# A graph network's edge blocks: the masks-times-weights products move to GpSimd, and two PSUM evictions to VectorE

## What is computed

```
z = _ln(x, ln1_g, ln1_b)
q = (z @ Wq + bq).reshape(L, H, D)
k = (z @ Wk + bk).reshape(L, H, D)
v = (z @ Wv + bv).reshape(L, H, D)
scores = einsum('ehd,ehd->eh', q[row], k[col]) * scale + bias
p = exp(scores - m[row])
alpha = p / segment_sum(p, row)[row]
out = segment_sum(alpha[:, :, None] * v[col], row)
```

## Time and profile before

| | before |
|---|---|
| median of 3 runs (lowest, highest) | 395.43 us (393.89, 395.63) |
| profiled execution, first to last instruction | 394.1 us |
| PE busy | 374.8 us, 95% |
| DVE busy | 312.1 us, 79% |
| ACT busy | 171.6 us, 44% |
| POOL busy | 4.2 us, 1% |
| stretch 22.0 to 104.2 us (fixed groups) | PE 81.1 of 82.2 us busy, DVE 80.2 |

### The profile page before, as it was taken

How to read it: one execution, slowest core, us unless ns; L and a number is a source line. 1 busy time by engine, 2 the same in 40 slices (tenths; PEclk the granted TensorE clock), 3 DMA queues, 4 the chain that set the end, 5 groups by cost and what they waited for, 6 DMA issues and landing times.

```text
span 394.1 us, 5108 instructions
## 1 busy us (share of the span) xinstructions
PE 374.8 (95%) x1786; PEld 282.2 (72%) x1786; DVE 312.1 (79%) x660; ACT 171.6 (44%) x287; POOL 4.2 (1%) x19
## 2 busy tenths in 40 slices
PE   2989999999999999999999999999999999999994
PEld 1545566666657888887678788887588878787773
DVE  5889999999848789897868976698875788388236
ACT  5664666563044234244559533262363530145410
POOL 4000000000000000000000000000000000000000
PEclk9999999999999999999999999999999999999988
DMA  7602444343135000068200512200600050000002
GB/s 238 250 1 69 152 154 141 105 153 112 52 112 183 1 2 0 2 215 315 111 2 1 172 43 101 114 0 0 211 4 0 2 180 33 2 0 0 2 12 94
DMA packets 16360, 32.92 MB, mean 84 GB/s; under 512 B 1360, under 2 KB 1488, under 8 KB 16336
## 3 DMA queue, kind: packets, MB, share of 16 engines
q1 hardware_dynamic: 15744, 32.25, 23.9%
q10 hardware_dynamic: 592, 0.36, 0.3%
HBM read 21.07 MB, written 1.05 MB: 56 GB/s over the span
## 4 chain that ended last, share of the span: by engine, by line
PE 77%; DVE 14%; ACT 4%; issue 2%; DMA 1%; DVEq 0%; ACTq 0%
PE acc L1395 11%; PE bank L1377 10%; PE bank L1480 7%; PE bank L1270 6%; PE bank L1271 6%; PE bank L1251 4%; PE acc L1251 4%; PE acc L1271 4%; PE acc L1270 4%; PE bank L1465 3%; PE acc L1451 3%; DVE big_rounded L652 2%; PE acc L1228 2%; PE bank L1228 2%; PE acc L1545 2%
## 5 line engine op out<-in xcount | busy, mean ns | idle before, releaser
L1395 PE MATMUL acc<-wide_rounded,c_rounded 128*126 128x512 f32 x200 | 59.5, 439 | 0.7 <-ACT acc L464 0.7
L1395 PEld LDWEIGHTS acc<-wide_rounded,c_rounded 128*126 128x126 f32 x200 | 36.9, 186 | 19.8 <-issue 13.0
L792 DVE TENSOR_SCALAR wide_rounded<-iota_f,picked 128x512 fp32r<-128x512 f32 x100 | 42.2, 480 | 1.5 <-issue 1.1
L483 ACT COPY z_sb<-acc 126x512 f32<-126x512 f32 x37 | 21.6, 585 | 42.0 <-PE acc L1395 33.3
L507 ACT ACTIVATE wide<-wide,low_col 128x512 f32<-128x512 f32 x32 | 21.3, 715 | 32.9 <-DVE low_col L905 32.8
L1480 PEld LDWEIGHTS bank<-v_sb,big 128*128 128x128 f32 x256 | 29.7, 192 | 4.7 <-issue 4.0
L625 DVE TENSOR_TENSOR wslot_rounded<-wslot,wide_rounded 128x512 fp32r<-128x512 f32 x24 | 16.2, 687 | 21.2 <-ACT wslot L377 21.2
L1480 PE MATMUL bank<-v_sb,big 128*128 128x65 f32 x256 | 31.6, 277 | 0.0
L798 DVE TENSOR_TENSOR c_rounded<-row_bc,wslot_rounded 128x1008 fp32r<-128x1008 bf16 x25 | 30.0, 1201 | 0.0
L1377 PE MATMUL bank<-t_sb,wslot 128*128 128x512 f32 x64 | 29.5, 594 | 0.5 <-ACT t_sb L459 0.5
L652 DVE TENSOR_TENSOR big_rounded<-big,big_rounded 128x1024 fp32r<-128x1024 f32 x24 | 29.1, 1221 | 0.5
(11 more groups left out here) (312 smaller groups left out, 769.6 us busy)
## 6 DMA issues: line engine op xcount, KB each, us to landing
big<-z_sb SPq DMA_DIRECT2D x36, 252.0 KB
big<-in_w SPq DMA_DIRECT2D x4, 2048.0 KB, 7.8
x_sb<-in_x SPq DMA_DIRECT2D x8, 256.0 KB, 4.6
big<-in_w_3t SPq DMA_DIRECT2D x2, 1024.0 KB, 6.7
row_bc<-in_rows SPq DMA_DIRECT2D x7, 256.0 KB, 6.4
wslot<-in_wq SPq DMA_DIRECT2D x1, 1024.0 KB, 8.9
wslot<-in_wk SPq DMA_DIRECT2D x1, 1024.0 KB, 10.7
wslot<-in_wv SPq DMA_DIRECT2D x1, 1024.0 KB, 12.8
```

The costliest lines, as they stand in the source:

```text
L483: nc.scalar.copy(stage[0:BROWS, b % STAGES, :], a).then_inc(S["staged"], 1)
L792: nc.vector.tensor_scalar(hot_ring[:, u, k, :], iota_f[:, :], picked[:, 0, s0 + k:s0 + k + 1], None, ALU.is_equal)
L1395: last = nc.tensor.matmul(to, st_ring[:, u, 2 * k + a, :, :].rearrange("p w k -> p (w k)"), hot_ring[:, u, k, :], start=False, stop=False, ...
```

## The change

`left_sides` becomes a function of the engine. For the 24 fixed groups GpSimd calls it, one instruction per group, in a loop of its own at the end of its program; the last group's product in the loop stays on VectorE. PE waits for two counters in place of one (`hots` from VectorE, `lefts` from GpSimd). VectorE evicts tiles 2 and 3 of the turned input instead of ScalarE, so it does two `tensor_scalar` of 128x512 from PSUM.

```diff
+        MASK_STEPS = {0: 5, RING: 8, 6: 9}
+        def left_sides(engine, u, s0):
+            c = slice(s0, s0 + GROUP)
+            return engine.tensor_tensor(
+                st_ring[:, u, :, :, :],
...
@@ gpsimd
+            pool.wait_ge(S["tables"], 7 + NT)
+            for g in range(NG - 1):
+                if g in MASK_STEPS:
+                    pool.wait_ge(S["round_steps"], MASK_STEPS[g])
+                if g >= RING:
+                    pool.wait_ge(S["pair_mm"], (g - RING + 1) * GROUP + 1)
+                left_sides(nc.gpsimd, g % RING, g * GROUP).then_inc(S["lefts"], 1)
@@ scalar
             clear(Z_BANKS[0])
-            z_turned(2)
-            z_turned(3)
             clear(Z_BANKS[1])
@@ vector
+            def z_turned(t):
+                dve.wait_ge(S["turned"], t + 1)
+                nc.vector.tensor_scalar(t_sb[:, t, :], bank[Z_BANKS[t]][:, :], colp("ln1_g", t), colp("ln1_b", t),
+                                        ALU.mult, ALU.add).then_inc(S["t_vector"], 1)
...
-            one_hots(0, 0, (2, 3))
+            one_hots(0, 0, (2, 3)).then_inc(S["hots"], 1)
             ln_coefs(1)
             for t in (0, 1):
                 ln_plain(1, t, h_sb)
-            left_sides(0, 0)
             slot_weights(5, later)
             dve.sem_inc(S["weights_read"], 1)
-            build(1, 1, GROUP)
+            dve.wait_ge(S["cols_in"], 16)
+            for t in (2, 3):
+                z_turned(t)
+            one_hots(1, GROUP).then_inc(S["hots"], 1)
...
             for g in range(RING, NG - 1):
-                build(g, g % RING, g * GROUP, (g - RING) * GROUP)
+                one_hots(g % RING, g * GROUP, freed=(g - RING) * GROUP).then_inc(S["hots"], 1)
...
             with nc.vector.Fori(0, trips) as j:
-                build(NG - 1, 0, FIXED, j * GROUP + (FIXED - RING * GROUP))
+                one_hots(0, FIXED, freed=j * GROUP + (FIXED - RING * GROUP))
+                left_sides(nc.vector, 0, FIXED).then_inc(S["built"], 1)
@@ tensor
             for g in range(NG - 1):
-                pairs(g, g % RING, held[GROUP * (g % 2):GROUP * (g % 2 + 1)])
+                pe.wait_ge(S["hots"], g + 1)
+                pe.wait_ge(S["lefts"], g + 1)
+                pairs(g % RING, held[GROUP * (g % 2):GROUP * (g % 2 + 1)])
                 if g == 0:
-                    pe.wait_ge(S["t_ready"], NT)
+                    pe.wait_ge(S["t_ready"], 2)
+                    pe.wait_ge(S["t_vector"], 2)
```

More of the change, by code:

```diff
@@ L231, in gnn_kernel @@
             "x_sums", "z_scalar", "w_hi", "pick_zeros", "meets_ready", "ranks_mm", "ranks_ready", "ends_mm", "ends_ready", "rounds_ready", "slots_ready", "slots_mm",
-            "picks_ready", "rows_ready", "picks_mm", "weights_mm", "weights_read", "round_steps", "built", "pair_mm", "pair_steps",
+            "picks_ready", "rows_ready", "picks_mm", "weights_mm", "weights_read", "round_steps", "hots", "lefts", "built", "t_vector", "pair_mm", "pair_steps",
             "evacuated", "staged", "b_out0", "b_out1", "b_out2", "c2_in", "qkv_mm",
@@ L270, in blocks_out @@
             return 16 * sum(len(block_parts(i)) for i in range(k, b, STAGES))
+        MASK_STEPS = {0: 5, RING: 8, 6: 9}
[3 more added lines that the diff above has]
+                st_ring[:, u, :, :, :],
+                mask[:, c, :, :].rearrange("p s a w -> p (s a) w").unsqueeze(3).broadcast_to(
+                    [P, 2 * GROUP, BW, KW]),
+                wp[:, c, :, :].bitcast(F32).rearrange("p s a k -> p (s a) k").unsqueeze(2).broadcast_to(
+                    [P, 2 * GROUP, BW, KW]), ALU.mult)
         block = ctx.enter_context(nc.Block())
@@ L791, in one_hots @@
                         dve.wait_ge(S["pair_mm"], freed + (k + 2))
[L792 to L808, removed]
+                    ins = nc.vector.tensor_scalar(hot_ring[:, u, k, :], iota_f[:, :], picked[:, 0, s0 + k:s0 + k + 1],
+                                                  None, ALU.is_equal)
+                return ins
+            def z_turned(t):
+                dve.wait_ge(S["turned"], t + 1)
+                nc.vector.tensor_scalar(t_sb[:, t, :], bank[Z_BANKS[t]][:, :], colp("ln1_g", t), colp("ln1_b", t),
+                                        ALU.mult, ALU.add).then_inc(S["t_vector"], 1)
             def qkv_out(n):
@@ L861, in _ @@
                                            ).then_inc(S["ends_ready"], 1)
-            dve.wait_ge(S["cols_in"], 16)
             dve.wait_ge(S["bv_in"], 16)
@@ L875, in _ @@
             with nc.vector.Fori(0, trips) as j:
-                build(NG - 1, 0, FIXED, j * GROUP + (FIXED - RING * GROUP))
+                one_hots(0, FIXED, freed=j * GROUP + (FIXED - RING * GROUP))
+                left_sides(nc.vector, 0, FIXED).then_inc(S["built"], 1)
                 at = j * 6 + 9
-                dve.wait_ge(S["built"], j + NG)
+                dve.wait_ge(S["built"], j + 1)
                 step(at + 1, nc.vector.tensor_single_scalar(slot1[:, chunk], slot1[:, chunk], float(GROUP), ALU.add))
@@ L992, in _ @@
             for t in range(NT):
-                split_lo("ff_in", t, t_lo, t_at, ready=("t_ready", NT))
+                split_lo("ff_in", t, t_lo, t_at, ready=("t_ready", 2))
             weight_lo("w1_0", 3, 4)
@@ L1386, in choices, with pairs @@
                 return held
-            def pairs(g, u, held):
-                pe.wait_ge(S["built"], g + 1)
+            def pairs(u, held):
                 for k in range(GROUP):
@@ L1438, in _ @@
                 pe.sem_inc(S["pair_steps"], 1)
-                pairs(j + (NG - 1), 0, choices(FIXED))
+                held = choices(FIXED)
+                pe.wait_ge(S["built"], j + 1)
+                pairs(0, held)
                 pe.wait_ge(S["qkv_ready"], LAST_V[0])
@@ L1532, in _ @@
             product_in_parts(FF1_BANKS, weight("w1_0", NT), halves(t_at, t_lo), reads("ff_in"), "ff1_mm",
-                             group=FT, weight_lo="w1_0_lo", second=(S["t_ready"], 2 * NT), by_tile=NT,
+                             group=FT, weight_lo="w1_0_lo", second=(S["t_ready"], 2 + NT), by_tile=NT,
                              free={2: (S["rcnt_ready"], 1), 3: (S["dinv_ready"], 1)})
```

## The result

The changed kernel takes 404.71 us (median of 4 runs, 403.27 to 405.19) against 395.43; the ratio is 1.024, with a 95% interval of 1.021 to 1.027. It is slower, as forecast, by half of what was forecast. The profiled execution has a span of 403.7 us, 9.6 us over that of before, and took 405.19 us. So a device time lies 1.5 us above its span, not at most one as was said ahead of the prediction, and the profiled execution of before, with its span of 394.1 us, stands for a time of some 395.6.

What follows compares the result with a forecast made beforehand. PE and VectorE were taken as balanced, with mutually exclusive one-hots and GpSimd products as the new bound: +16.7 (groups) -0.6 (evictions) +3.2 (start) -0.3 (last group), about +19 us, giving 414 us on the median; range 399 to 436 us.

Steps and rivals of the forecast that it cites:

- What bounds the kernel: Stage of the groups: PE and VectorE are balanced, so of 28.8 us taken off VectorE only 1.2 us lie on the path.
- the start's 0.7 us: Ahead of the first q step: two evictions moved to VectorE let it begin earlier, forecast as -0.6 us.
- Exclusion: Stage of the groups: a fast VectorE one-hot and a GpSimd instruction block each other, +16.7 us over 16 groups.
- GpSimd's waiting: Shared SBUF ports: GpSimd also blocks while VectorE holds them; taken from the Trainium skill, with no size of its own.
- the product's length: Each product of 128x1008 on GpSimd: 2.3 us, with 1.5 and 3.3 us kept for the range.
- the sum per group: From group 7 to 23: one-hots 1.67, product 2.3 and about 0.1 us make 4.1 us, against 3.58 and 2.72.
- changes of hand: Each group: two switches between one-hots and GpSimd's product, about 0.1 us in all.
- The Trainium skill's price: GpSimd's product: 4497 ns for a two-input operation over 2048 elements, an estimate of 2.2 us; the sum would hardly move.
- rival 1: Stage of the groups: exclusion with a cheap product of 1.5 us, about +6 us, 401 us; chance 0.18.
- the lead of two buffers: Early groups: 3.0 us of slack, 1.3 us left after queued one-hots, gone some three groups after group 4.
- The start: Ahead of the groups: GpSimd's first products hold one-hots and layer norm, +3.2 us, less 0.6 us from the moved evictions.

Runs made afterwards that it cites:

- warm: The whole change with 26 instead of 8 matmuls on a constant ahead of the transposes of z: 404.67 us, ratio 1.026.

## Why the prediction was right in direction and twice too large

*What bounds the kernel.* The change did not gain from relieving VectorE, but no run relieves it without giving GpSimd work, so that this would bring next to nothing is not shown by itself. Both attempts to win the start's 0.7 us with the products on VectorE ended at the ratio 1.00.

*Exclusion* is shown, from both sides: add an unread product and the one-hots are held; put the one-hots in the slow form and no one-hot is held, with the same product beside them, while the operations that stayed in the fast form still are. GpSimd's waiting, of which no row was there, shows too: 2.25 us at most in the changed kernel, 2.99 beside VectorE's product.

*The term that was mis-sized is the product's length, and with it the sum per group.* I took 2.3 us by proportion from the affine select; it is 1.97. In the terms of the prediction the sum is then 1.67 + 1.97 + 0.1 = 3.7 us and not 4.1, and the 0.1 for changes of hand did not show: from group 7 to group 13 the changed kernel needs 21.4 us, as before, where I had +3.2. One-hots and product, 1.6 + 1.97 = 3.6 us, are PE's own pace there. What the stage lost, it lost at groups 4 to 6 (+1.1 us, for which I had nothing; see *Open*) and behind group 13: +6.6 us up to group 23, where I had +13.5, and 0.3 at the last group. In place of +16.7 the stage lost 8.1 us. The Trainium skill's price (an estimate of 2.2 us) was nearer to the mark than mine, and as its sentence said, it would hardly have changed the sum.

What happened is thus rival 1 by its mechanism, hidden in the early stretch and paid in the late one, which had a chance of 0.18 and gave 401 us. The 404.71 us lie just below the 405 to 425 of the forecast, and inside the range only because that took in rival 1's cheap product. That the stated range holds the time is in part luck.

*A second error went the same way:* every group was to pay the full sum of 4.1 us. In fact the late groups run in bursts. PE keeps its pace of 2.72 us for two or three groups while VectorE falls behind, then waits 1.7 or 2.0 us once. The period over the late groups is (118.09 - 81.30) / 11 = 3.34 us. Two things can make it less than 3.6: a product held VectorE for 1.76 us and not for its whole 1.97, and the lead of two buffers is used up over these groups. Their shares were not measured.

*The start* was +3.4 us at group 1 against +2.6 forecast, by the route described: a one-hot, then the layer norm's coefficients behind the second product (I had named `ln_plain`; it was the tiny `shift`). The clock, which I had left out of the sum, adds to it: with the clock at 1.00, group 1 starts 1.0 us earlier. But the start's worth was misjudged: two experiments took its loss away wholly or in part, and the time stayed. What comes earlier into a stage that waits for VectorE waits there.

*Open:* why the 11 early products cost 1.8 us when the sum equals PE's pace. Their trace shows a part of it. Beside the first product `ends_u` took 1.67 us, so ScalarE's first block copy came at 30.05 instead of 28.80 us, and groups 4 and 6 started late (44.84 and 52.42 us). The experiment that handed the ends over earlier had group 4 on time, so a late accumulator is the likely cause. But at group 13 only 0.4 us are lost there and at group 23 1.2 us, so most of the cost appears in late groups, whose products VectorE makes itself; a lead that is gone by then would explain it, which I did not test. Nor did I try a product of another length, to see the threshold of 3.57 us directly.

## What to carry to other kernels

Before moving work from VectorE to GpSimd, ask what form VectorE's remaining work takes. A fast one-source operation from SBUF to SBUF waits for the end of the GpSimd instruction, and so does one with two SBUF inputs if GpSimd reads: here the moved instruction of 1.20 us kept VectorE waiting for 1.4 to 1.8 us. What was not held in these traces were one-hots in the slow form and the operations that read PSUM (the four of L829 on q took 750 to 751 ns each in the changed kernel). No run here shows the move paying; by these runs it could only where VectorE's remaining work is of those kinds, or where another engine is clearly the bound. And count the pace of each stretch: the same move cost 0.16 us per product where PE needed 3.57 us per group and 0.6 us where it needed 2.72.

## What the runs showed that I had not expected

- Slower instructions can make the faster kernel: one-hots of 744 ns instead of 476 took 3 to 4 us off the changed kernel.
- The smallest instruction pays in full. `shift` on 128x4 took 1.63 us and `ends_u` on 1x37 took 1.61 us beside a product.
- VectorE's hold on GpSimd is short in the changed kernel (at most 0.3 us on 1.95 us), where what stands in the way is a one-hot of 0.48 us; GpSimd's hold on VectorE lasts up to a whole product.
- In the changed kernel one wait of 2.0 us was followed by a granted clock of 0.54 for 3.6 us; in the trace of *warm* PE waited 2.1 us twice and the clock stayed at 1.00.
